# Causal 16-wide attention: the order of score products, maxima and V's products within a step

## The reference

```
q, k, v = split(layernorm(x) @ w_attn + b_attn + 2 * (layernorm(x) @ la @ lb))   # 16 heads of width 16
k, v = fake_quant(k), fake_quant(v)
scores = einsum('bhqd,bhkd->bhqk', q, k) / 4
scores = where(causal, scores, -inf)
out = einsum('bhqk,bhkd->bhqd', softmax(scores), v)
x = x + (out @ w_proj + b_proj + 2 * (out @ la_proj @ lb_proj))
```

## Time and profile before

| | |
|---|---|
| Time, median of 3 runs | 2941.66 us (2934.39 to 2953.08) |
| The profiled execution | 2941.67 us, span 2940.0 us |
| Granted TensorE clock, mean of the span | 0.813 |
| TensorE, VectorE, ScalarE, GpSimd busy | 72%, 58%, 34%, 30% of the span |
| Causal attention, first to last score product | 106.4 us to 420.8 us |

### The profile page before, as it was taken

How to read it: one execution, slowest core, us unless ns; L and a number is a source line. 1 busy time by engine, 2 the same in 40 slices (tenths; PEclk the granted TensorE clock), 3 DMA queues, 4 the chain that set the end, 5 groups by cost and what they waited for, 6 DMA issues and landing times. The chain is left out here.

```text
span 2940.0 us, 37771 instructions
## 1 busy us (share of the span) xinstructions
PE 2102.9 (72%) x13657; PEld 1074.0 (37%) x13661; DVE 1707.5 (58%) x3086; ACT 1003.4 (34%) x1732; POOL 881.1 (30%) x1057
## 2 busy tenths in 40 slices
PE   7688878776579965699999862443757594439992
PEld 4233335224322233133333331221333263327992
DVE  4667735665368753577777335997583705335442
ACT  3377751321023312377777411111110120134330
POOL 2122212110223312746474110233271201152225
PEclk9699979778789977699999856555878697569996
DMA  5100000000100003211010122000111100153113
GB/s 176 40 23 23 23 8 18 1 1 10 26 1 1 1 17 133 76 29 33 24 32 23 33 73 64 2 2 5 56 43 39 34 0 4 57 190 102 44 52 97
DMA packets 81055, 118.55 MB, mean 40 GB/s; under 512 B 17957, under 2 KB 57905, under 8 KB 79857
## 3 DMA queue, kind: packets, MB, share of 16 engines
q1 hardware_dynamic: 72289, 104.29, 11.0%
q0 software_dynamic: 3664, 9.32, 1.1%
q10 hardware_dynamic: 4928, 2.62, 0.3%
HBM read 78.65 MB, written 37.29 MB: 39 GB/s over the span
## 5 line engine op out<-in xcount | busy, mean ns | idle before, releaser
L1283 DVE TENSOR_REDUCE a_mneg<-a_SM 128x1 f32<-128x1024 f32 x256 | 302.5, 1220 | 123.1 <-PE a_SM L1145 122.2
L1266 ACT ACTIVATE a_P<-a_ST 128x512 f32<-128x512 f32 x512 | 290.8, 596 | 127.5 <-PE a_ST L1176 122.5
L924 ACT ACTIVATE a_P<-a_ST,a_scale 128x512 f32<-128x512 f32 (+3 forms) x384 | 206.3, 588 | 85.3 <-PE a_ST L836 83.5
L939 DVE TENSOR_REDUCE a_mx<-a_SM 128x2 f32<-128x1024 f32 (+1 forms) x192 | 176.3, 952 | 67.9 <-PE a_SM L801 37.8
L1145 PE MATMUL a_SM<-a_K,a_Q 96*128 96x512 bf16 x512 | 161.8, 399 | 56.3 <-POOL a_V L1097 54.4
L1176 PE MATMUL a_ST<-a_Q,a_K 98*128 98x512 bf16 x512 | 179.0, 390 | 10.1 <-ACT a_P L1266 6.1
L771 POOL TENSOR_SCALAR_AFFINE_SELECT a_P<-a_P 128x128 f32<-128x128 f32 (+1 forms) x256 | 77.1, 306 | 243.9 <-ACT a_P L924 242.8
L1194 PE MATMUL a_OP<-a_P,a_V 128*32 128x512 f32 x1024 | 137.5, 609 | 0.9 <-ACT a_P L1266 0.7
L836 PE MATMUL a_ST<-a_Q,a_K 50*128 50x512 bf16 (+3 forms) x384 | 119.6, 360 | 24.0 <-ACT a_P L924 23.6
L3274 DVE TENSOR_TENSOR experts_hl<-work 128x512 bf16<-128x512 f32 x92 | 83.8, 969 | 87.8 <-POOL work L3124 87.8
L3124 POOL CAST work<-work 128x512 bf16<-128x512 f32 x92 | 73.9, 841 | 197.9 <-PE experts_py L3208 184.6
(11 more groups left out here) (546 smaller groups left out, 4923.6 us busy)
## 6 DMA issues: line engine op xcount, KB each, us to landing
work<-L_ffn_W SPq DMA_DIRECT2D x16, 1024.0 KB, 5.1
conv_tab<-dft_tables SPq DMA_DIRECT2D x8, 1024.0 KB, 4.9
bias_hankel<-bias_rows SPq DMA_DIRECT2D x16, 448.0 KB, 3.5
a_Q<-q_stacks SPq DMA_DIRECT2D x16, 384.0 KB, 3.9
a_K<-k_stacks SPq DMA_DIRECT2D x16, 384.0 KB, 4.7
expert_rows<-zeros SPq DMA_DIRECT2D x1, 5888.0 KB, 23.1
experts_xs<-expert_rows SPq DMA_DIRECT2D x23, 256.0 KB, 2.9
expert_results<-params SPq DMA_DIRECT2D x23, 256.0 KB, 2.2
```

Source lines behind the costliest of these rows:

```text
L924: act.activation(Pr[:, s % 2, u, j, c0:N], ST[:, u, c0:N], ACT.Exp, scale=kscale[:, 0:1]).then_inc(exp_done, 1)
L939: dve.tensor_reduce(mx[:, g % 2, qt, k0 // N, :], SM[:, c % 2, :, 0:kn], AX.X, ALU.max).then_inc(mx_read, 1)
L1266: act.activation(Pr[:, s % 2, u, j, c0:N], ST[:, (4 * s + x) % 2, c0:N], ACT.Exp, scale=scale).then_inc(exp_done, 1)
L1283: dve.tensor_reduce(mneg[:, g % 2, u, qt:qt + 1], SM[:, c % 2, 0:width(qt)], AX.X, ALU.max, negate=True).then_inc(mx_read, 1)
```

## The change

The loop over steps in TensorE's program is written in another order. Score products go in pairs, 0 and 1, then 2 and 3; the first of the step's two chunks of maxima stands between the pairs (with `rows` behind it where the step has one), `values` of the step before and `outputs` follow the fourth score product, and the second chunk is last. The programs of the other engines are as before.

```diff
--- before
+++ after
@@ -878,20 +878,19 @@
                 for s in range(NG * ns):
                     lo, hi = done, chunks_by(s)
                     done = hi
-                    cut = [lo + (hi - lo + 2) // 3, lo + 2 * (hi - lo + 1) // 3]
+                    cut = lo + (hi - lo + 1) // 2
                     scores(s, 0)
-                    maxima(lo, cut[0])
+                    scores(s, 1)
+                    maxima(lo, cut)
                     if event(rows_at, s):
                         rows(*event(rows_at, s))
-                    scores(s, 1)
-                    maxima(cut[0], cut[1])
                     scores(s, 2)
+                    scores(s, 3)
                     if s:
                         values(s - 1)
                     if event(outputs_at, s):
                         outputs(*event(outputs_at, s))
-                    scores(s, 3)
-                    maxima(cut[1], hi)
+                    maxima(cut, hi)
                 values(NG * ns - 1)
                 outputs(NG - 1, 1)
```

## The result

The changed kernel takes 3066.81 us (median of 4 runs, 3045.76 to 3078.36) against 2942.09 us (4 runs, 2934.39 to 2953.08): ratio 1.0409, 95% interval 1.0346 to 1.0472. It is slower; the forecast was 3040 us with a range of 2985 to 3105. The profiled execution of the changed kernel took 3078.36 us, the longest of its four, so what is read from it lies above the median.

What follows compares the result with a forecast made beforehand. Bound: attention's loop of TensorE score products and ScalarE exponentials through two PSUM buffers. Onto 2941.66 us came 57 us of loop and stall (2999), then 42 us of lost clock (3041), stated as 3040 us, range 2985 to 3105.

Steps and rivals of the forecast that it cites:

- The fourth score product ahead of V's: Attention loop, steps 0 to 4: V's products no longer run beside the first exponentials; 1.96 us more a group.
- Chunk 11's chain to L820: Step 5: the rows' products wait for VectorE's work on the late last chunk; 1.74 us more a group.
- The smaller wait for the bank in step 2: Step 2: L820 held until about 1.2 us by the result of step 1's outputs, beside the loop; costs nothing.
- the rows' later DMAs: Row DMAs go out later by L820's delay, with 4 us needed of some 7 us of room; costs nothing.
- Pairs, nothing gained: Score products in different row halves already overlapped with a chunk's product, so pairing them gains nothing.
- The sum without the clock: Attention stage: groups of 22.40 us instead of 18.70, 57 us in all, giving 2999 us.
- The clock, a third of the stage: TensorE busy 74% loses its full clock part of the time; a third of 125 us, taken as 42 us.
- The price of a group at 0.50: A full attention group in the new order at half clock takes 32.0 us, 9.6 us over 22.4.
- (a): Rival: the stall costs time in attention but the clock stays as now; 2985 to 3010 us, chance 0.27.
- (b): Rival: the clock in attention is mostly at 0.50; 3090 to 3124 us, chance 0.13.
- (c): Rival: only the loop costs, L820 not held by chunk 11's chain; 29 us, 2950 to 2971 us, chance 0.09.
- (d): Rival: TensorE's time decides, pairs run together and fill its 2.17 us a group; 33 us less, 2909 us, chance 0.06.

Runs made afterwards that it cites:

- filled_three_steps: The changed kernel plus unused TensorE products, 12 in step 5 and four in each of steps 1 and 3 of a group: 2988.83 us, ratio 1.0176.
- chunk_before_v: The changed kernel with the step's second chunk of maxima moved back ahead of V's products, behind the fourth score product: 3019.68 us, ratio 1.0286.
- result_first: The changed kernel with VectorE doing the result of the outputs ahead of the second chunk's reduction, TensorE's order untouched: 3106.44 us, ratio 1.0570.
- changed_filled: The changed kernel with 12 unused TensorE products added in step 5 of 14 groups, ahead of the first chunk: 3024.40 us, ratio 1.0276.
- pairs_only: The kernel before with only the second score product moved up next to the first: 2974.52 us, ratio 1.0126.
- filled_steps_1_3: The changed kernel with four unused TensorE products in each of steps 1 and 3, none in step 5: 3014.33 us, ratio 1.0255.
- rows_behind_v: The changed kernel with the rows' products behind V's and the outputs, and ScalarE's copy of the rows behind the step's last exponential: 3104.45 us, ratio 1.0557.

## Why the prediction was right, and where it was off

**The fourth score product ahead of V's, 1.96 us a group**: right. Steps 0 to 4 at full clock were predicted at 2.96, 4.00, 2.85, 3.80 and 4.35 us and are 2.96, 4.03, 2.85, 3.82 and 4.35 in filled_three_steps: 18.01 us together, 2.01 more than the 16.00 before. chunk_before_v, whose second chunk stands elsewhere but whose products stand in the same order, has 20.60, 1.90 over the group before. It could be laid out because the units came from rows of the same shapes.

**Chunk 11's chain to L820, 1.74 us a group**: right. 2.93 us from its issue to the rows against 3.05; step 5 took 4.28 against 4.44, so 1.58 more than the 2.70 before, and the two terms come to 3.60 where the prediction had 3.70. That the result stands in this chain was shown by result_first: with it moved, the wait is 0.53 us shorter.

**The smaller wait for the bank in step 2, nothing, and the rows' later DMAs, nothing**: right. In changed_filled the rows of step 2 start 1.18 us into it (1.2 predicted), and step 2 has its 2.85 us; no wait for a row DMA stands in the list of waits of filled_three_steps.

**Pairs, nothing gained**: right for the change, but pairs alone cost something that the text didn't say. pairs_only has 19.21 us a group. Within the sum this cost was contained, since the steps were laid out with both products ahead. The Trainium skill has it that matmuls of few rows in different row groups run at once ("TensorE: Matmul & The Clock Gate", Why this matters for your kernels). The rows agree about that, as the prediction read at 279.16, but the overlap was in use before the change: no order with pairs in every step had a shorter group.

**The sum without the clock, 57 us**: measured 50. filled_three_steps is 49.97 us above the kernel before by the medians (2988.83 against 2938.86), 49.7 in the stage of the two traces (364.1 against 314.4). The steady group was 22.40 by the prediction and is 22.30. The 7 us between 57 and 50 are in groups 0 and 1, for which the prediction had 2 x 4.5: they took 25.0 and 22.3 us against 24.4 and 22.8 before, with more clock (0.71 and 1.00 against 0.50 and 0.73), so next to nothing. The last group, level in the prediction, took 1.5 us more, 25.3 at 0.50 against 23.8 at 0.62. Groups 9 and 14 (23.0 and 23.2, both at 0.93) are inside the 50.

**The clock, a third of the stage, 42 us**: the mis-sized term. Its sign was right. By the medians it is 3066.81 - 2988.83 = 78 us, by the two ratios 2.3% or 68 us. In the profiled execution it is 138.0 - 49.7 = 88. The price of a group at 0.50 was good: 32.0 predicted, and the one full group at 0.50 in filled_steps_1_3 took 31.90 (with 0.4 us of filling in each of two steps). The share was wrong: the steady groups 1 to 8 at 0.56 spend seven eighths of their time at the lower clock, and the mean of the stage is 0.63. The step that failed is the sentence "I take a third, 42 us, since no row says how quickly it comes back". The busy shares that led there, 88% kept and 82% lost, gave a direction and no size, and the experiments show that they carry neither: 81% keeps the clock in one order, 90% loses it in another, and rows_behind_v sits at 0.50 with 91%. That the direction came out right is partly luck. The two errors have opposite signs, 7 us too much in the sum and 26 to 46 too little for the clock, and left the forecast 27 us short.

**Two smaller points of the working.** The 32.0 us for a group at 0.50 came out right, but the prediction names three of its units and doesn't lay it out. And the chances above 2971 us come to 0.85 (0.45, 0.27 and 0.13), not 0.87.

**The rivals.** (a), the clock as now, 2985 to 3010: not what happened, but it is what filled_three_steps is, 2989. (b), mostly 0.50, 3090 to 3124: the clock's level in groups 1 to 8 is nearer to this one than to the forecast, and rows_behind_v and result_first end in its range (3104 and 3106). The time of the change itself, 3067, fell in the forecast's own band of 3010 to 3090, between 3040 and (b). (c), only the loop: excluded by the 2.15 us at L820; its period of 20.6 us is that of chunk_before_v. (d), faster: excluded, no shared time was won.

What stays open is what TensorE has to do for the clock to stay. In this order, filling the waits brings it back; in chunk_before_v it did not help, and in the kernel before it did harm. No run here says why.

## What to carry to other kernels

Lay the loop of two engines out along the order, step by step, with durations of the same shapes from the timeline: this gave steps 0 to 4 to 0.03 us, for a change that moves no instruction between engines. Before moving work ahead of a reader, count what stands between a chunk and the first instruction that reads it, on every engine in its chain and in the bank that they share. And a new wait on TensorE can cost twice, once by itself and once by the clock (50 and some 78 us here), without the busy share telling which kernels lose it: give the clock a term of its own, with bounds wide enough for all of the stage. Filling the wait with unused products shows what the lost clock is worth in that kernel; it is no remedy to count on, since it made the kernel before slower.

## What the runs showed that I had not expected

- Twenty unused products a group, 180 records instead of 156 to 160, made the changed kernel 78 us faster (3066.81 to 2988.83), although TensorE is the engine that everything waits for.
- The clock was lost without any long wait: in chunk_before_v the longest idle time ahead of the fall is 0.68 us, and half of its stage is below 1.00.
- The same filling made the kernel before 35 us slower (2976.47 against 2941.55), of which only some 15 us are the products themselves (19.8 - 18.7 us in 14 groups); the rest is clock, lost at a higher busy share than before.
- The clock repeats with the group. The changed kernel stayed at 30.8 us for eight groups in a row and rises once in each near its start; result_first, with a shorter wait, missed that rise in four of thirteen groups and took 31.4.
